# Linear attention of a decoder layer: query and key biases as one pass of 64 rows, and the next pair's input transposed one step earlier

## The reference

```python
q = x @ Wq.T + bq
k = x @ Wk.T + bk
v = x @ Wv.T + bv
q = jax.nn.softplus(to_z(q))
k = jax.nn.softplus(to_z(k))
kv = jnp.cumsum(k[:, :, :, None] * v[:, :, None, :], axis=1)
k1 = jnp.cumsum(k, axis=1)
num = jnp.einsum('zsD,zsDe->zse', q, kv)
den = jnp.sum(q * k1, axis=-1, keepdims=True)
out = num / den
return out @ Wo.T + bo
```

## Time and profile before

| | |
|---|---|
| median of three runs | 2255.25 us |
| profiled execution, its own time | 2259.26 us |
| span of its profile | 2257.3 us |
| busy share of the span | PE 96%, PEld 82%, DVE 69%, ACT 62%, POOL 61% |
| end of the linear attention in the profile | about 309 us |

### The profile page before, as it was taken

How to read it: one execution, slowest core, us unless ns; L and a number is a source line. 1 busy time by engine, 2 the same in 40 slices (tenths; PEclk the granted TensorE clock), 3 DMA queues, 4 the chain that set the end, 5 groups by cost and what they waited for, 6 DMA issues and landing times. The chain is left out here.

```text
span 2257.3 us, 44552 instructions
## 1 busy us (share of the span) xinstructions
PE 2164.8 (96%) x16235; PEld 1847.5 (82%) x16235; DVE 1548.4 (69%) x3425; ACT 1395.0 (62%) x3756; POOL 1372.0 (61%) x1481
## 2 busy tenths in 40 slices
PE   6899968999999999999999999999989999999998
PEld 3555547999999999999999999999977777777776
DVE  3799955666666666666666666666657777777775
ACT  3455535666666676666766666666745665665664
POOL 4688846565565665655655656656644666666666
PEclk9999979999999999999999999999999999999999
DMA  3311100000000000000000000000000000000000
GB/s 100 111 34 32 32 24 6 11 6 6 11 6 6 11 6 9 8 6 11 6 6 10 6 6 10 6 6 10 6 1 1 10 5 10 10 6 11 10 6 15
DMA packets 52794, 33.40 MB, mean 15 GB/s; under 512 B 3096, under 2 KB 50274, under 8 KB 52450
## 3 DMA queue, kind: packets, MB, share of 16 engines
q1 hardware_dynamic: 50174, 26.30, 4.0%
q10 hardware_dynamic: 2404, 4.26, 0.7%
HBM read 22.16 MB, written 8.39 MB: 14 GB/s over the span
## 5 line engine op out<-in xcount | busy, mean ns | idle before, releaser
L660 POOL TENSOR_TENSOR x_prob<-x_prob,x_inv 128x496 f32<-128x496 f32 x514 | 520.8, 1013 | 548.9 <-DVE x_inv L799 548.8
L735 ACT ACTIVATE x_prob<-x_ps_S,x_nmax 128x248 f32<-128x248 f32 x1028 | 473.3, 467 | 131.0 <-DVE x_nmax L793 131.0
L793 DVE TENSOR_REDUCE x_nmax<-x_ps_S 128x2 f32<-128x496 f32 x515 | 345.5, 671 | 182.8 <-PE x_ps_S L498 182.5
L743 ACT COPY x_probT<-x_ps_T 124x512 f32<-124x512 f32 x512 | 300.4, 587 | 226.3 <-PE x_ps_T L962 226.3
L1124 POOL TENSOR_TENSOR e_hidden_lo<-e_hidden,e_hidden_hi 128x512 fp32r<-128x512 f32 x224 | 291.2, 1303 | 198.4 <-ACT e_hidden_hi L1168 197.6
L496 PE MATMUL x_ps_S<-x_kT_lo,x_G_hi 128*128 128x248 f32 x1030 | 329.8, 320 | 0.0
L962 PE MATMUL x_ps_T<-ident,x_prob 128*124 128x128 f32 x2048 | 314.8, 276 | 11.7 <-POOL x_prob L660 11.7
L962 PEld LDWEIGHTS x_ps_T<-ident,x_prob 128*124 128x124 f32 x2048 | 237.6, 139 | 72.0 <-POOL x_prob L660 29.5
L497 PE MATMUL x_ps_S<-x_kT_hi,x_G_lo 128*128 128x248 f32 x1030 | 287.2, 279 | 0.0
L498 PE MATMUL x_ps_S<-x_kT_hi,x_G_hi 128*128 128x248 f32 x1030 | 286.8, 278 | 0.0
L779 DVE TENSOR_TENSOR x_G_lo<-x_ps_G,x_G_hi 128x512 fp32r<-128x512 f32 x259 | 178.8, 690 | 130.0 <-ACT x_G_hi L729 129.9
(11 more groups left out here) (199 smaller groups left out, 5015.4 us busy)
## 6 DMA issues: line engine op xcount, KB each, us to landing
x_nk<-latents SPq DMA_DIRECT2D x34, 124.0 KB
lin_x_rows<-in_x SPq DMA_DIRECT2D x32, 128.0 KB, 2.3
latents<-lin_nlat SPq DMA_DIRECT2D x32, 128.0 KB, 1.8
out_dram<-e_result SPq DMA_DIRECT2D x16, 256.0 KB, 2.2
x_nk<-in_ctx SPq DMA_DIRECT2D x34, 120.0 KB, 2.2
w_wkv<-in_L_xattn_Wkv SPq DMA_DIRECT2D x1, 1024.0 KB, 6.2
w_rows<-in_L_ffn_w_gate SPq DMA_DIRECT2D x1, 704.0 KB, 5.9
w_rows<-in_L_ffn_w_up SPq DMA_DIRECT2D x1, 704.0 KB, 6.2
```

What stands on the lines that cost most here:

```text
L660: nc.gpsimd.tensor_tensor(prob[:, k], prob[:, k], inv[:, k].unsqueeze(2).broadcast_to([P, 2, K]), ALU.mult).then_inc(prob_ready, 1)
L735: nc.scalar.activation(prob[:, k, h, :], ps_S[:, n % BANKS, h * K:(h + 1) * K], ACT.Exp, bias=nmax[:, k, h:h + 1], accum_out=total[:, k, h ...
L743: nc.scalar.copy(probT[0:KT, s % (2 * GANG)], ps_T[0:KT, s % 2, :]).then_inc(probT_ready, 1)
L793: nc.vector.tensor_reduce(nmax[:, k, :], ps_S[:, n % BANKS, 0:2 * K].rearrange("p (h k) -> p h k", h=2), AX, ALU.max, negate=True).then_in ...
```

## The change

The two bias rows (high and low part) and their duplicate for the second sequence become one operand of 64 partitions and 512 columns. Row 0 holds the high part; row 32 the low part; all others are zero. One product with 64 rows of ones puts the whole bias of both sequences into `ps_qk`, in place of four products of one row and 256 columns. To fill the operand POOL clears it first, ACT issues four small DMAs in place of two and waits for that clearing, and DVE rounds a 64 x 512 tile.

On PE the two transposes of x leave the head of the step. A function `turn_rows` issues them for pair 0 ahead of all steps, and for pair t+1 within step t, behind L464 and L469 and ahead of L479 and L486.

```diff
+    LOW = 32
+    ROWS = 64
-        b_qk = room.sbuf("b_qk", [1, QK])
-        b_qk_part = [room.sbuf(f"b_qk_{n}", [1, QK], F32R) for n in ("hi", "lo")]
+        b_qk = room.sbuf("b_qk", [ROWS, 2, QK])
+        b_qk_parts = room.sbuf("b_qk_parts", [ROWS, 2, QK], F32R)
-        ones = room.sbuf("ones", [1, P], F32R)
+        ones = room.sbuf("ones", [ROWS, P], F32R)
@@ POOL
+            nc.gpsimd.memset(b_qk[:], 0.0).then_inc(zero_ready, 1)
@@ ACT
-            for n in range(2):
-                act.dma_start(b_qk[:, n * D:(n + 1) * D], biases[n].rearrange("(o d) -> o d", o=1)
-                              ).then_inc(bqk_loaded, 16)
+            act.wait_ge(zero_ready, 1)
+            for row in (0, LOW):
+                for n in range(2):
+                    act.dma_start(b_qk[row:row + 1, :, n * D:(n + 1) * D],
+                                  biases[n].rearrange("(o u d) -> o u d", o=1, u=1).broadcast_to([1, 2, D])
+                                  ).then_inc(bqk_loaded, 16)
@@ DVE
-            dve.wait_ge(bqk_loaded, 32)
-            nc.vector.tensor_copy(b_qk_part[0][:], b_qk[:]).then_inc(b_hi_ready, 1)
+            dve.wait_ge(bqk_loaded, 64)
+            nc.vector.tensor_copy(b_qk_parts[:], b_qk[:]).then_inc(b_hi_ready, 1)
             dve.wait_ge(b_hi_ready, 1)
-            nc.vector.tensor_tensor(b_qk_part[1][:], b_qk[:], b_qk_part[0][:].bitcast(F32), ALU.subtract
+            low = slice(LOW, LOW + 1)
+            nc.vector.tensor_tensor(b_qk_parts[low], b_qk[low], b_qk_parts[low].bitcast(F32), ALU.subtract
                                     ).then_inc(b_lo_ready, 1)
@@ PE
+            def turn_rows(t, par):
+
+                wait(pe, aT_ready, t - 3)
+                pe.wait_ge(x_loaded[par], landed(t, par))
+                for u in range(2):
+                    last = nc.tensor.transpose(ps_t[:, u * S:(u + 1) * S], x_rows[:, par, u, :], ident[:])
+                last.then_inc(xT_psum, 1)
+
+            turn_rows(0, 0)
+
             def step(t, par):
                 s1, s3 = t - 1, t - 3
                 if here(t):
-                    wait(pe, aT_ready, s3)
-                    pe.wait_ge(x_loaded[par], landed(t, par))
-                    for u in range(2):
-                        last = nc.tensor.transpose(ps_t[:, u * S:(u + 1) * S], x_rows[:, par, u, :], ident[:])
-                    last.then_inc(xT_psum, 1)
                     pe.wait_ge(xT_ready, t + 1)
                     wait(pe, pos_ready, t)
+                    nc.tensor.matmul(ps_qk[:], ones[:], b_qk_parts[:].rearrange("p u f -> p (u f)"), start=True, stop=False)
                     for u in range(2):
-                        out = ps_qk[:, u * QK:(u + 1) * QK]
-                        nc.tensor.matmul(out, ones[:], b_qk_part[1][:], start=True, stop=False)
-                        nc.tensor.matmul(out, ones[:], b_qk_part[0][:], start=False, stop=False)
-                        last = nc.tensor.matmul(out, turned[:, u, :], w[:, 0:QK], start=False, stop=True)
+                        last = nc.tensor.matmul(ps_qk[:, u * QK:(u + 1) * QK], turned[:, u, :], w[:, 0:QK], start=False,
+                                                stop=(u == 1))
                     last.then_inc(qk_psum, 1)
...
                 if here(t) or here(s3):
                     last.then_inc(vy_psum, 1)
+                if here(t + 1):
+                    turn_rows(t + 1, 1 - par)
                 if here(s1):
 
                     pe.wait_ge(qk_ready, s1 + 1)
```

More of the change, by code:

```diff
@@ L208, in linear_attention @@
         half_ready, ones_ready = room.sem("half_ready"), room.sem("ones_ready")
-        b_hi_ready, b_lo_ready = room.sem("b_hi_ready"), room.sem("b_lo_ready")
+        b_hi_ready, b_lo_ready, zero_ready = room.sem("b_hi_ready"), room.sem("b_lo_ready"), room.sem("zero_ready")
         xT_psum, xT_ready = room.sem("xT_psum"), room.sem("xT_ready")
```

## The result

| | before | changed |
|---|---|---|
| median | 2255.57 us (2255.05 to 2259.59, 6 runs) | 2267.95 us (2265.79 to 2270.17, 6 runs) |
| ratio to before | 1 | 1.005 (95% interval 1.0037 to 1.0063) |
| span of the profiled execution | 2257.3 us | 2268.3 us |
| cross-attention's first load starts at | 310.97 us | 325.12 us |

The changed kernel is slower: by 12.4 us between the medians, by 11.3 us by the ratio; 6.1 had been forecast. The six executions of the kernel before lie in two groups (2255.05 to 2255.89 and 2259.47 to 2259.59), so the difference is known to some 3 us. In the two profiles linear attention alone ends 14.15 us later (325.12 - 310.97). What follows it takes 1946.3 us before and 1943.2 after, but that share does not follow the change: it takes 1942 to 1943.2 or 1945.3 to 1946.3 in the thirteen profiles of this study, whatever the first stage looks like.

A forecast was written before the change was run, and what follows sets the result against it. PE, with a detour over ACT, was taken to bound the kernel. +1.4 us up to pair 5, +5.3 in 24 steps and -0.6 after the last transposes gave +6.1 on 2255.25, rounded 2261.5 us; range 2246 to 2272.

The forecast's parts named there:

- What bounds the kernel now: In the steady stretch, PE with one detour over ACT sets the 8.13 us step; DVE alone would need 7.49.
- What the change takes from PE: Per steady step, bias passes save 0.43 us and transposes 0.63, leaving PE 7.07 us, less than DVE's 7.49.
- The new loop: Each step, PE's early transposes wait for a load behind a store which that step feeds; 8.35 us.
- 24 steps: From the L365 at 82.70 on, 24 steps have the longer loop: 24 x (8.35 - 8.13) = +5.3 us.
- Rival 3: TensorE's clock falls to 1.2 GHz in PE's pauses: up to 56 us, 2315; a few such steps, 2270; chance 4%.
- the named signs of being wrong: Steady stretch: period near 7.5, DVE never idle; clock under 1.00 from 100 to 280 us; DMA wait without L365 starting later.
- Early part: Up to pair 5's L365, start costs, early gains and the weights' stall together: +1.4 us, 2 us either way.
- (a): Start: POOL's clearing, about 0.5 us, and two more DMA issues at 0.4 each delay the loads; +1.0 us taken.
- (b): Steps 0 and 1: one bias pass for four saves 1.0 us in each, transposes add 0.44; -1.6 us.
- (c): Steps 3 and 4, whose loads have no store before them, fall from 8.12 towards 7.49 us; -1.5 us in both.
- The step after the last transposes: Near the end of the loop, this step falls to DVE's 7.49 us: -0.6 us.
- Rival 1: DVE sets the steady step at 7.49 us, as the load's wait does not end last; 2238 us, chance 15%.

The follow-up runs named there:

- e1: The changed kernel with SP issuing the load of pair t ahead of the store of pair t-5 instead of behind it; 2251.91 us.
- e2: The changed kernel with the next pair's transposes between the two halves of the running sums instead of ahead of L492; 2249.37 us.
- e3: The changed kernel's moved transposes, with the four bias passes, their operands and loads of the kernel before; 2268.09 us.
- e6: The changed kernel with one more small unused DMA issued by SP between store and load, from pair 5 on; 2272.41 us.
- e8: The changed kernel with the four small bias DMAs issued by SP behind the four weights instead of by ScalarE; 2264.18 us.
- e4: The changed kernel's single bias pass and start, with the transposes where the kernel before has them; 2249.84 us.
- e5: The kernel of e2 with GpSimd adding b_o into X behind its two products instead of ahead of them; 2242.77 us.

## Why the prediction was right, and where its sizes were off

- **What bounds the kernel now**: right. PE with a detour over ACT, DVE 0.6 us behind.
- **What the change takes from PE**: transposes right. The bias pass took 0.42 us (0.43 taken), but the bias part saved 0.63, not 0.43, because the products behind it became 0.20 shorter. It had no weight in the time, as PE waits in each step.
- **The new loop**: right, shown by e1 and e2, which open it at either end, by e3, which has it alone, and in part by e6. Forecast 8.35 us, measured 8.36 in steps at full clock; from the load's issue to the transposes 2.44 us on average (8.36 less the 5.92 of the shown step's other terms), 2.45 taken. PE's wait was 1.1 us on average (1.2 forecast) and DVE's 0.9 (0.86), both without the slow step.
- **24 steps**: +5.3 forecast, 203.18 - 195.18 = +8.0 measured (195.18 is 24 x 8.1325, the period from the earlier trace rows). The difference is the one step with a late landing and a slow clock, 10.85 - 8.36 = 2.5 us. Rival 3 was real, in one step of 24, and with it one of the named signs of being wrong, a granted clock under 1.00 between 100 and 280 us. The row used against it (a pause of 2.15 us without a fall) was a single case; here 1.89 us came before a fall, while waits of 1.75 us in the same run (transposes at 269.91), 1.80 in e6 and 1.82 in e8 came before none. The length of the last wait alone does not tell. The Trainium skill, "TensorE: Matmul & The Clock Gate", section "A second HAM failure mode: psum-queue depth-cycling", on short pauses between groups of matmuls, was cited for that rival; it is borne out only in this weak form: one fall in 24 steps. That rival's price has a slip: 56 us on top of the 2261.5 give 2317, not 2315.
- **Early part**: the term of the sum that was mis-sized. (a) +1.0 taken, +3.0 measured (22.02 - 19.02): the four bias issues on ScalarE cost 1.24, 0.59, 0.56 and 0.56 us, not 0.4, and nothing of it hid behind the loads of X. e8 gives 3.8 us back. (b) and (c) about right, though (c) takes 1.5 where two times 8.12 - 7.49 is 1.3: L372 of pair 0 is only 35.16 - 34.01 = 1.15 us later after a start 3.0 later (34.01 is that instruction in the trace of before), and that of pair 2 at 49.04 is 0.35 earlier than before. Because the 3 us ate these gains, the store of pair 0 was issued at the old time (52.39, before 52.42), not 2.3 us earlier. PE restarted after the weights at 72.88 and not at 70.5, and pair 5 was +3.56, not +1.4.
- **The step after the last transposes**: -0.6 forecast, 296.80 - 289.44 = 7.36 against 8.13, -0.77. Not foreseen: in the drain PE stands 3.16 us instead of 2.15 and the clock falls there, +2.7 us. That PE stands longer because it has less work is an inference. The last step took 10.05 us here and 10.06 in e1 and e6, but 8.93 in e3, 9.11 in e4 and e8, and 7.87 in e2.
- **Rival 1's price**: wrong. DVE alone does not need 7.49 us but 7.87, once it is no longer held back, since its shift then meets POOL's addition. Its time would have been near 2250 us, as e1 and e2 show, not 2238. It didn't decide, but three expectations (e1, e2, e4) inherited the error.

In the profile: +3.56 up to pair 5, +8.0 in 24 steps, -0.77, +2.7, +0.7 behind it, 14.15 in all. The range of 2246 to 2272 held, and the new loop's own range, 2256 to 2268, just held; the size was forecast at half. The loop's 8.35 us was worked out; that the start, the slow step and the drain together did not lead out of the range is in part luck, as no term of the forecast stood for the last two.

## What to carry to other kernels

When an instruction that waits for a transfer is moved forward on an in-order engine, follow the transfer back to its issue: if that issue stands in its queue behind something which the moved instruction's own step feeds, a loop closes, and the issue and landing of the transfer are in it. The time to spare of a load is read at its new place, not at the old one. And taking a limit's idle time as the gain is an upper bound: work that used to be apart starts to overlap when the waiting ends.

## What the runs showed of the hardware that was not expected

VectorE and GpSimd hold each other up over instructions that read two operands from SBUF: 0.68 us for a 128 x 4 operation that takes 0.15 alone, 1.24 for one of 0.73, both gone when e5 moves one of them. The Trainium skill, "SBUF — State Buffer", section "SBUF: two separate sides", describes this as an exclusive lock held for a whole instruction, not a shared bandwidth. The rows agree: L384 runs its usual 0.68 us, POOL's addition ends 0.58 us after it (less than its own 0.73, so part of it had run or was hidden), and L390 ends with the addition, 0.02 us apart. L423, with one operand from SBUF, was stretched too in e5 (0.40 for 0.18) and ended 0.02 us after POOL's `att`; no run takes that pair apart, so its cause is not shown.

A small DMA is not cheap to issue. One row of 2 x 128 numbers, read twice from the same 128, cost ScalarE 0.56 to 1.24 us of issue and SP 0.56 to 0.72 (e8). A load of 128 x 256 numbers cost SP 0.47, and a plain row of 128 cost ScalarE 0.53 and 0.22 in the kernel before and SP 0.27 in e6.
